# Gated block, last feed-forward: the rounding step's limit on ScalarE, another order of half tiles on VectorE, row turns placed among the down products

## What is computed

```python
def _mx_dequant(t):                      # blocks of 32 along the last dimension
    blocks = t.reshape(rows, feat // 32, 32)
    max_abs = jnp.max(jnp.abs(blocks), axis=-1)
    scales = jnp.maximum(max_abs / 448.0, 1e-30)
    q = (blocks / scales[..., None]).astype(jnp.float8_e4m3fn).astype(jnp.float32)
    return (q * scales[..., None]).reshape(rows, feat)

def _mx_linear(x2d, w):
    return _mx_dequant(x2d) @ _mx_dequant(w).T

gate = _mx_linear(x2d, gate_w)           # (1024, 256) by (256, 1024)
up = _mx_linear(x2d, up_w)
h = jax.nn.silu(gate) * up
out = _mx_linear(h, down_w)              # (1024, 1024) by (1024, 256)
...
x = x + jnp.tanh(g_ffn[1]) * _L1_ffn_ref(_layernorm(x, axis=-1), gate_w, up_w, down_w)
```

## Time and profile before

| | before |
|---|---|
| median of 3 runs | 458.1 us (455.8 to 459.13) |
| profiled execution, its own time | 451.05 us |
| its span in the trace | 449.3 us |
| PE busy | 386.7 us (86%) |
| DVE busy | 331.0 us (74%) |
| POOL busy | 243.0 us (54%) |
| ACT busy | 184.6 us (41%) |
| mean granted TensorE clock | 0.939 of full |

### The profile page before, as it was taken

How to read it: one execution, slowest core, us unless ns; L and a number is a source line. 1 busy time by engine, 2 the same in 40 slices (tenths; PEclk the granted TensorE clock), 3 DMA queues, 4 the chain that set the end, 5 groups by cost and what they waited for, 6 DMA issues and landing times.

```text
span 449.3 us, 8497 instructions
## 1 busy us (share of the span) xinstructions
PE 386.7 (86%) x2886; PEld 272.9 (61%) x2886; DVE 331.0 (74%) x744; ACT 184.6 (41%) x435; POOL 243.0 (54%) x344
## 2 busy tenths in 40 slices
PE   7678987899999998869969889888879999889865
PEld 6456765778766655545538567666644555545544
DVE  3768989873575888885832487886677999999990
ACT  2463966214454466663725333454341212211120
POOL 5556667537776777673116588742042645554441
PEclk9898989989999999995977977999989999999996
DMA  7799969744279989999754334431000000000000
GB/s 240 252 261 225 209 146 198 212 94 100 90 212 289 308 200 298 203 177 183 186 163 125 100 119 131 130 107 50 1 1 0 0 12 14 12 12 1 12 12 23
DMA packets 71527, 57.42 MB, mean 128 GB/s; under 512 B 38070, under 2 KB 63804, under 8 KB 71484
## 3 DMA queue, kind: packets, MB, share of 16 engines
q1 hardware_dynamic: 66864, 44.28, 35.9%
q0 software_dynamic: 4608, 12.59, 13.0%
q10 hardware_dynamic: 12, 0.00, 0.0%
HBM read 42.18 MB, written 14.68 MB: 127 GB/s over the span
## 4 chain that ended last, share of the span: by engine, by line
PE 37%; DVE 23%; issue 17%; POOL 12%; ACT 5%; DMA 4%; DVEq 1%; POOLq 0%; ACTq 0%
PE psum L1403 8%; PE psum L1414 5%; POOL arena_dn L741 4%; PE psum L1621 3%; PE psum L1638 3%; PE psum L1422 3%; POOL mx_w L744 3%; DMA ys_dram<-stage 3%; PE psum L1679 2%; PE psum L1705 2%; PE psum L1794 2%; PE psum L1806 2%; DVE arena_dn L1245 2%; DVE arena_up L1305 2%; DMA shared<-h_dram,tok_u 1%
## 5 line engine op out<-in xcount | busy, mean ns | idle before, releaser
L626 POOL DMA_INDIRECT shared<-h_dram,tok_u x60 | 59.6, 993 | 20.5 <-issue 13.6
L1736 PE MATMUL psum<-arena_dn 128*128 128x512 f32 x128 | 57.1, 598 | 3.2 <-ACT arena_dn L895 3.2
L741 POOL TENSOR_TENSOR arena_dn<-arena_dn 128x512 f32<-128x512 f32 x16 | 20.3, 1270 | 45.7 <-DVE arena_dn L1210 45.7
L1638 PE MATMUL psum<-arena_dn,h1T 64*64 64x256 f32 x256 | 37.3, 412 | 7.1 <-issue 4.8
L1736 PEld LDWEIGHTS psum<-arena_dn 128*128 128x128 f32 x128 | 23.7, 190 | 31.2 <-issue 26.3
L679 POOL DMA_INDIRECT arena_up<-ys_dram,slot_u x32 | 31.3, 979 | 15.0 <-issue 7.8
L1403 PE MATMUL psum<-ident,arena_up 128*128 128x128 f32 x144 | 25.3, 294 | 12.8 <-DVE arena_up L1044 6.1
L1414 PE MATMUL psum<-h1T,shared 128*128 128x256 f32 x128 | 32.6, 404 | 1.2 <-ACT arena_up L772 1.2
L1831 PE MATMUL psum<-arena_dn,mx_w 128*128 128x256 f32 x128 | 31.2, 400 | 0.4 <-ACT mx_w L905 0.3
L1403 PEld LDWEIGHTS psum<-ident,arena_up 128*128 128x128 f32 x144 | 17.2, 148 | 22.3 <-DVE arena_up L1044 9.0
L1403 PE MATMUL psum<-ident,mx_w 128*128 128x128 f32 x128 | 21.6, 300 | 9.5 <-POOL mx_w L744 8.8
(11 more groups left out here) (239 smaller groups left out, 942.0 us busy)
## 6 DMA issues: line engine op xcount, KB each, us to landing
ys_dram<-stage SPq DMA_DIRECT2D x32, 256.0 KB, 5.5
arena_up<-in_L_ffn_wg_dram SPq DMA_DIRECT2D x8, 512.0 KB, 5.1
arena_up<-in_L_ffn_wu_dram SPq DMA_DIRECT2D x8, 512.0 KB, 6.6
arena_dn<-in_L_ffn_wd_dram SPq DMA_DIRECT2D x64, 64.0 KB
va_dram<-stage SPq DMA_DIRECT2D x8, 256.0 KB, 4.7
kT_dram<-stage SPq DMA_DIRECT2D x8, 256.0 KB, 2.7
arena_dn<-in_L_ffn_wd_dram SPq DMA_DIRECT2D x2, 1024.0 KB, 8.4
arena_dn<-in_L_ffn_wd_dram SPq DMA_DIRECT2D x4, 512.0 KB, 8.7
```

Of the source, the lines that this page charges most:

```text
L626: pool.indirect_dma_start(out=xg_at(n)[:, b, :], out_offset=None, in_=h1_dram[:, :], in_offset=bass.IndirectOffsetOnAxis(ap=tok_u[:, 2 * n ...
L741: pool.tensor_tensor(haF[h], haF[h], heF[h], ALU.subtract).then_inc(sem("hint"), 1)
L1638: ins = pe.matmul(bank[6 + n % 2][at, b * D:(b + 1) * D], hbT[n % 2][0:F, b, at], w, start=True, stop=True)
L1736: ins = pe.matmul(bank[2 * part + h][:, :], xTF[n % 2][:, c, :], mx_gu[:, c, lo:lo + HW], start=(c == 0), stop=(c == C - 1))
```

## The change

The limit from below leaves DVE. With LIMIT = FP8_TINY * ROUND4, ACT forms relu(ROUND4 * e - LIMIT) in place of e (`limit`, its first activation), and in a second activation adds LIMIT to get the whole number (hmF for halves, xmF for a row). DVE's last step becomes one instruction that adds the step, LIMIT and the value (`rounded`); POOL subtracts the whole number. The rows 0 and 1 still use the old way. The two pointers of ACT come from a small constant tile `limc` that POOL writes.

The order is rewritten on four engines. DVE: the exponents of a half (`half_scale`) and its closing addition (`rounded`) are apart, with the gate product of the other half between; the last addition of tile n-1 (`row_final`) and the rounding of row n+2 (`row_scale`) stand at the end of a turn of the loop. ACT: the limits stand between silu and copies. PE: the turn of row n+2 stands after five of the eight down products of tile n. POOL: the same steps in another order, and not the last half of tile 7: DVE closes that one in two quarters of 256 columns, PE turns each quarter by itself into banks 7 and 5, and has four filler products (`keep_warm`, into bank 3) before them.

```diff
-            def half_quant(n, h):
+            def exponents(src, width, mx, sc, rs, y, e):
...
+                dve.tensor_scalar(e.bitcast(U32), y.bitcast(U32), EXPONENT, None, ALU.bitwise_and).then_inc(sem("expo"), 1)
+
+            def rounded(a, e, y, last):
+                limits[0] = limits[0] + 1
+                dve.wait_ge(sem("limit"), 2 * limits[0] - 1)
+                dve.scalar_tensor_tensor(a, e, LIMIT, y, ALU.add, ALU.add).then_inc(sem(last), 1)
...
+            for n in range(T):
+                if n:
+                    half_gate(n, 0)
+                    if n + 1 < T:
+                        rounded(xaF, xeF, xyF, "xround")
+                    half_scale(n, 0)
+                half_gate(n, 1)
+                rounded(haF[0], heF[0], hyF, "hround")
+                half_scale(n, 1)
+                if n + 3 < T:
+                    row_sums(n + 3)
+                rounded(haF[1], heF[1], hyF, "hround")
+                if n:
+                    row_final(n - 1)
+                if n + 2 < T:
+                    row_scale(n + 2)
+            reach(dve, sem("hTF_ps"), 2 * T - 4)
+            for c in range(2):
...
+                chain(dve.tensor_tensor(haF[1][:, at], haF[1][:, at], hmF[1][:, at], ALU.subtract), "r")
...
+            row_final(T - 1)
```

ScalarE:

```diff
+            def limit(step, whole):
+                limits[0] = limits[0] + 1
+                act.wait_ge(sem("expo"), limits[0])
+                act.activation(step, step, ACT.Relu, bias=limc[:, 0:1], scale=ROUND4).then_inc(sem("limit"), 1)
+                act.wait_ge(sem("limit"), 2 * limits[0] - 1)
+                act.activation(whole, step, ACT.Identity, bias=limc[:, 1:2]).then_inc(sem("limit"), 1)
+
+            limits = [0]
+            act.wait_ge(sem("pad"), 10)
             gate(0, 1)
-            for k in range(1, T + 1):
-                if k < T:
-                    row_out(k)
+            for n in range(T):
+                if n:
+                    gate(n, 0)
+                    if n + 1 < T:
+                        limit(xeF, xmF)
+                    gate(n, 1)
+                limit(heF[0], hmF[0])
+                if n == 0:
+                    row_out(1)
+                else:
                     for h in range(2):
-                        gate(k, h)
-                for h in range(2):
-                    hidden_out(k - 1, h)
+                        hidden_out(n - 1, h)
+                limit(heF[1], hmF[1])
+                if 1 < n + 1 < T:
+                    row_out(n + 1)
+            hidden_out(T - 1, 0)
```

GpSimd and TensorE:

```diff
+            for n in range(T):
+                if 2 <= n + 1 < T:
+                    row_close(n + 1)
+                half_close(n, 0)
+                if n + 3 < T:
+                    row_root(n + 3)
+                if n < T - 1:
+                    half_close(n, 1)
...
+            gate_up(0, 1)
+            row_turn_q(1)
+            for n in range(T):
+                if n + 1 < T:
+                    for h in range(2):
+                        gate_up(n + 1, h)
+                    for h in range(2):
...
+                        half_turns(n, h, range(4), 6 + h)
...
+                    down_parts(n, range(5))
+                    if n + 2 < T:
+                        row_turn_q(n + 2)
+                    down_parts(n, range(5, 8)).then_inc(sem("dF"), 1)
...
+            down_parts(n, range(4))
+            pe.wait_ge(sem("hF"), 2 * T)
+            keep_warm(4, 3)
+            for c in range(2):
+                pe.wait_ge(sem("hround"), 2 * T + 1 + c)
...
+                half_turns(n, 1, range(2 * c, 2 * c + 2), 7 - 2 * c)
+            down_parts(n, range(4, 6))
+            pe.wait_ge(sem("hTF"), 2 * n + 3)
+            down_parts(n, range(6, 8)).then_inc(sem("dF"), 1)
```

More of the change, by code:

```diff
@@ L339, in build_program @@
         haF = [take(HW) for _ in range(2)]
+        hmF = [take(HW) for _ in range(2)]
+        xmF = take(D)
         take = carver(mx_w)
@@ L663, in _ @@
             for b in range(2):
+                pool.memset(limc[:, b:b + 1], LIMIT if b else -LIMIT).then_inc(sem("pad"), 1)
+            for b in range(2):
                 pool.memset(qn[b][:, :, HD:HP], 0.0).then_inc(sem("pad"), 1)
@@ L748, in _, with row_root, row_close @@
-            run_steps(pool, T, 2, 2, ffn_pool, lead=T)
+            ints = [0]
+            def row_root(n):
+                b = n % 2
+                inv_sqrt(rstd[:, b:b + 1], mv[:, b, 1:2], LN_EPS, "mvE", T + n + 1, "rstdF")
+            def row_close(n):
+                pool.wait_ge(sem("xround"), n + 1)
+                if n >= 2:
+                    pool.wait_ge(sem("limit"), 6 * (n - 1))
+                pool.tensor_tensor(xaF, xaF, xmF if n >= 2 else xeF, ALU.subtract).then_inc(sem("int"), 1)
+                ints[0] = ints[0] + 1
+                pool.wait_ge(sem("int"), ints[0])
+                reach(pool, sem("xTF_ps"), n - 1)
+                xq, sc = xqF[n % 2].rearrange(b3, w=QB), amc.unsqueeze(2).to_broadcast([P, D // QB, QB])
+                pool.tensor_tensor(xq, xaF.rearrange(b3, w=QB), sc, ALU.mult).then_inc(sem("xqF"), 1)
@@ new lines, in half_close @@
+            def half_close(n, h):
+                pool.wait_ge(sem("hround"), 2 * n + h + 1)
+                pool.wait_ge(sem("limit"), 2 * (2 * n + h + 1 + min(n, T - 2)))
+                pool.tensor_tensor(haF[h], haF[h], hmF[h], ALU.subtract).then_inc(sem("int"), 1)
+                ints[0] = ints[0] + 1
+                pool.wait_ge(sem("int"), ints[0])
+                reach(pool, sem("hTF_ps"), 2 * n + h - 3)
+                pool.tensor_tensor(hqF[n % 2][:, h * HW:(h + 1) * HW].rearrange(b3, w=QB),
+                                   haF[h].rearrange(b3, w=QB),
+                                   ahc[h].unsqueeze(2).to_broadcast([P, HW // QB, QB]), ALU.mult)\
+                    .then_inc(sem("hqF"), 1)
@@ L1320, in row_quant, with link @@
                 quantise(xnF[s], D, amx, amc, arc, xyF, xeF, xaF, "xround")
-            def half_quant(n, h):
+            limits = [0]
+            b3 = "p (b w) -> p b w"
+            def exponents(src, width, mx, sc, rs, y, e):
+                def link(ins):
+                    chain(ins, "r")
+                link(dve.tensor_reduce(mx, src.rearrange(b3, w=QB), AX.X, ALU.max, apply_absolute_value=True))
+                link(dve.tensor_scalar(sc, mx, 1.0 / FP8_MAX, 1e-30, ALU.mult, ALU.max))
+                link(dve.reciprocal(rs, sc))
+                link(dve.tensor_tensor(y.rearrange(b3, w=QB), src.rearrange(b3, w=QB),
+                                       rs.unsqueeze(2).to_broadcast([P, width // QB, QB]), ALU.mult))
+                dve.tensor_scalar(e.bitcast(U32), y.bitcast(U32), EXPONENT, None, ALU.bitwise_and).then_inc(sem("expo"), 1)
@@ L1330, in _, with row_final @@
+            def row_final(n):
+                dve.wait_ge(sem("dF"), n + 1)
+                dve.scalar_tensor_tensor(x_res[:, n, :], bank[4][:, 0:D], tg[:, GF1:GF1 + 1], x_res[:, n, :],
+                                         ALU.mult, ALU.add).then_inc(sem("x4"), 1)
             for k in range(-2, T + 2):
@@ L1374, in _ @@
                 if k == T + 1:
[L1375 removed]
+                    half_gate(0, 0)
+                    half_scale(0, 0)
                 if 0 <= c < T:
```

115 lines of the change are left out of this document (54 added, 61 removed).

## The result

| | before | after |
|---|---|---|
| median of four runs each, new runs of before among them | 456.95 us (454.6 to 459.13) | 465.6 us (463.06 to 467.54) |
| ratio after to before | | 1.0216 (95%: 1.0162 to 1.0271) |
| profiled execution: own time, span | 451.05, 449.3 us | 467.54, 465.8 us |
| gate and up of tile 1 to the end of the span | 105.3 us | 115.3 us |
| gate and up of tile 1 to that of tile 2 | 12.7 us | 21.15 us |

The changed kernel is slower by 8.65 us between the medians. Its profiled execution is the slowest of its four, and that of the kernel before was faster than all of its four; so the two profiles are 16.5 us apart. Of these, 6.5 lie ahead of tile 1's gate and up (350.51 against 343.98), nearly all of it before tile 0's, in the part that both kernels share. The rest is 8.4 at the start and 5.9 in the middle, less 4.35 at the end: 10.0.

What follows compares the result with a forecast made beforehand. It took DVE and PE as near each other before, and a dependence ring through PE, DVE and ACT after. Span 449.3 + 12.6 - 4.3 + 2.0 = 459.6, own time 461.35, median 468.4 us; range 457 to 473.

Steps and rivals of the forecast that it cites:

- The tile: Middle of the kernel, tile 2 to tile 7: a tile takes 14.2 us, against 13.19 before.
- The hold: A DVE instruction stands until POOL's ends, by their shared port pair; second half's small scale 0.57, multiply 0.60 us.
- the ring: Dependences through PE, DVE, ACT and PE, closed by ACT's row copy behind the second half's limit; its length sets the tile, 14.2.
- DVE's last addition and the row part lie beside this: In each tile, these DVE steps were taken to add nothing to the 14.2 us.
- The forecast's own sign against itself: In the changed profile, the prediction is wrong if DVE still has no gap or PE waits for nothing at gate and up.
- (a): Rival: POOL and DVE don't meet, 13.2 a tile as before, start loses 2.8, 457.3 us in all; chance 0.15.
- (b): Rival: PE's floor of 12.25 a tile holds from the start, 8.8 us less, 449.3; chance 0.07.
- (c): Rival: half the holds, no clock fall in tile 1, 13.7 a tile, some 4 to 5 us more, 462 to 463; chance 0.14.
- (d): Rival: the clock falls in each tile, 2 us more for each of six tiles, 480 us; chance 0.04.
- The start: Up to tile 2: late first limit loses 6.7 us, PE stands 352.8 to 358.8, and a clock fall adds 2.0.
- The end: Gate and up of tile 7 to the span's end: 23.1 to 23.2 against 27.5 us, 4.3 gained, fillers included.
- The sum: Whole kernel: span 459.6, own time 461.35 against 451.05, 10.3 us more, median 468.4; chance 0.60.

Runs made afterwards that it cites:

- Opening the ring: Changed kernel with ScalarE's row copy ahead of the second half's limit: 14.00 us for each of three tiles, middle 69.3 against 71.0 us.
- GpSimd was short: Changed kernel with GpSimd's four closing instructions per tile on their first 32 columns only: 12.88 us a tile, 104.7 us from tile 1 on.
- the opened order: Changed kernel with GpSimd's closes on 32 columns, row copy before the second limit, hidden copies between the first limit's activations: 12.13 us a tile, 97.7 in all.

## Why the prediction was right, and where not

**The tile.** Right at every station, counted from gate and up at 399.99: first product 3.80 (forecast 3.77), mask of the first half over at 7.34 (7.30), addition 8.13 (8.13), second maximum 8.74 (8.74), second multiply 10.61 (10.55), its mask over at 12.39 (12.29), row copy 13.81 (13.76), next gate and up 14.21 (14.2). The copies of the halves let the down products start at 9.46 (9.5). The hold on the scale was 0.66 (0.57), on the multiply 0.63 (0.60), on the first half 0.2 (0.2). An activation of limit took 0.72 (0.70).

**What the tile would be without the ring.** Here the working failed: "DVE's last addition and the row part lie beside this". They do, but with 0.34 to spare. The row part alone has holds of 1.08 on L1389 and 0.34 on its scale, which the forecast priced at the start but nowhere in a tile, and with them DVE by itself closes a tile at 14.0. The forecast's own sign against itself, that DVE still has no gap, was nearly met: its gaps are 0.8 a tile, two of the three of them waits for limits. Opening the ring as a remedy gave 0.2, not the 0.8 that PE waits there. The new order alone, with the limit on DVE, gave 14.15. So the forecast of 14.2 rested on one of two bounds that happen to agree; that the one it left out lay 0.2 lower, and not higher, was luck.

**Rivals.** (a) put the tile without holds at 13.2; it was 12.88 when GpSimd was short. The rival didn't come about, much as was said against it: the subtract L750 starts 0.25 after the second half's maximum in every tile of the middle. What releases it by the profile is ACT's second activation, though, which ends at 408.84, 0.03 after the addition that the forecast named. (b) put PE's floor at 12.25; the opened order came to 12.13, with 0.48 of waiting still in it. (c) took half the holds and a clock that stays in tile 1; the holds came whole, and the clock fell. Its own terms add up to 3.8 more, not 4 to 5. (d) didn't come about: stops of 1.46 and 0.83 in each tile left the clock at full (ten down records 2.40).

**The start.** 21.15 measured, 21.4 forecast, both by the late first limit and one fall of the clock; PE stood 5.67 for the 6.0 forecast. With the limit back on VectorE the start was 13.9, which bears the late limit out. That the start also hangs on the holds (17.3 with GpSimd short, 14.85 with the ring opened too) the forecast had only in part.

**The end.** 23.15 measured, 23.1 to 23.2 forecast, with one term wrong: "of it 2.05 by a clock that the fillers keep at 2.4 GHz". Without fillers the clock stayed as well, in one profile, and PE's longest stop in that end is 1.09; the fillers cost 1.7, which the sum had as work of PE's and set against a loss that didn't come. That the total was right here although this reason was not is luck.

**The sum.** 10.3 forecast; 10.0 in the profile's stretch, 8.65 between the medians. The interval of the ratio, 7.4 to 12.4 us of 456.95, holds both. The median came to 465.6, where the forecast was 468.4: 1.15 of the 2.8 is the base, whose median is 456.95 with the new run and was 458.1 without it. The other 1.65 lies in no term that the runs single out. The fall of the clock at the start isn't it by what the profiles show: the four other runs with that start have it too (21.2, 21.4, 20.8 and 21.2).

## What to carry to other kernels

Where VectorE and GpSimd share the work on SBUF data, count VectorE's load with the time it stands behind GpSimd: an order that gives each engine less to wait for can still cost more if it puts GpSimd's long instructions on VectorE's two-input ones. A dependence ring laid out station by station gave the time of a tile to 0.1 us here, but before it is used to say what a remedy brings, lay out the next ring and the full engine as well. An end can be shortened by itself. Before adding work that is to keep a clock up, look which stops are there: the fillers cost 1.7 where no stop was longer than 1.09, and where one of 1.93 was, it came from an addition that stood too late in VectorE's queue.

## What the runs showed of the hardware that was not expected

- The hold takes small instructions whole: a scale of 16 values per partition, 0.17 by itself, took 0.84 behind a 512-wide subtract on GpSimd, and a normalising of 256 took 1.48 for 0.40. The maxima of 512 columns (0.68 to 0.69) and the product with an input in PSUM (0.68 to 0.69) kept their times in every run. That a maximum never contends with GpSimd on this chip, and an instruction with one input in SBUF only in the two-port modes, is what the Trainium skill has (SBUF — State Buffer, Who interferes with whom), and the trace agrees. With GpSimd's instructions at 32 columns no hold was left, before or after the change.
- Stops of about the same length had different outcomes for the granted clock. After 5.67 it was at 0.50; after 3.10, in the run with the ring opened, down products ran at the full rate (2.40 for ten records); after 1.93 and 1.94 it fell in two profiles (3.12 and 3.26 for eight records), and after 1.93 it stayed in a third (1.99), of nearly the same kernel as the first. Within one profile, a stop of 2.43 kept it in one tile (2.40 for ten records) and lost it in the next (3.50). What decides between these, the runs don't settle.
